# Three bias buffers, three probability buffers, and the transposes and products one unit earlier in an attention kernel

## The reference, cut to what matters

```python
# x: (16, 1024, 256), 16 heads of 16
Q, K, V = x @ Wq.T, x @ Wk.T, x @ Wv.T                 # each split into heads
rel_k, rel_v = pek[idx], pev[idx]                      # idx = clip(j - i, -256, 256) + 256
scores = (Q K^T + einsum('bhqd,qkd->bhqk', Q, rel_k)) / 4
attn = softmax(where(causal, scores, -inf))
out = attn V + einsum('bhqk,qkd->bhqd', attn, rel_v)
x = layernorm(x + out @ Wo.T)
x = layernorm(x + (silu(x @ wg.T) * (x @ wu.T)) @ wd.T)
```

## Time and profile before

| | |
|---|---|
| median of 3 runs | 5551.6 us (5548.85 to 5560.93) |
| profiled execution, its own time | 5554.04 us |
| its span | 5552.3 us |
| attention stage | about 417 to 4338 us of the span |
| TensorE, VectorE, ScalarE, GpSimd busy | 92%, 68%, 62%, 33% of the span |
| DMA | 1417.28 MB, mean 255 GB/s |

### The profile page before, as it was taken

How to read it: one execution, slowest core, us unless ns; L and a number is a source line. 1 busy time by engine, 2 the same in 40 slices (tenths; PEclk the granted TensorE clock), 3 DMA queues, 4 the chain that set the end, 5 groups by cost and what they waited for, 6 DMA issues and landing times. The chain is left out here.

```text
span 5552.3 us, 143052 instructions
## 1 busy us (share of the span) xinstructions
PE 5135.0 (92%) x49460; PEld 3335.1 (60%) x49460; DVE 3756.9 (68%) x8777; ACT 3432.3 (62%) x7512; POOL 1832.5 (33%) x2516
## 2 busy tenths in 40 slices
PE   9987999999999999999999999999999799999999
PEld 5554666666666666666666666666666465665655
DVE  4555777777777777777777777777777455555554
ACT  4446787877878778777877877787777211111111
POOL 3444333333333333333333333333333111111111
PEclk9998999999999999999999999999999899999999
DMA  7888999999999999999999999999999311111110
GB/s 225 253 254 265 318 321 320 327 320 324 326 323 322 324 325 317 326 318 317 324 324 318 324 319 318 320 324 324 320 317 312 106 61 52 54 60 60 60 54 33
DMA packets 653784, 1417.28 MB, mean 255 GB/s; under 512 B 64004, under 2 KB 362088, under 8 KB 640872
## 3 DMA queue, kind: packets, MB, share of 16 engines
q1 hardware_dynamic: 653160, 1409.10, 78.2%
HBM read 737.46 MB, written 671.35 MB: 254 GB/s over the span
## 5 line engine op out<-in xcount | busy, mean ns | idle before, releaser
L797 ACT ACTIVATE a_prob<-a_neg_s,a_neg_max 128x384 f32<-128x384 f32 (+1 forms) x1792 | 1083.3, 605 | 231.1 <-DVE a_neg_max L846 215.1
L761 PE MATMUL a_t_ps<-a_ident,a_prob 128*128 128x128 f32 x5120 | 927.8, 281 | 41.7 <-DVE a_p_t L515 28.7
L515 DVE COPY a_p_t<-a_t_ps 128x512 f32<-128x512 f32 (+3 forms) x1536 | 952.6, 620 | 6.7 <-PE a_t_ps L761 5.5
L694 PE MATMUL a_s_ps<-a_k,a_q 96*128 96x512 bf16 (+3 forms) x3072 | 853.4, 332 | 111.5 <-ACT a_far L801 106.6
L840 DVE TENSOR_REDUCE a_far_neg<-a_s_ps 128x1 f32<-128x640 f32 (+4 forms) x1280 | 707.6, 553 | 367.4 <-POOL a_bias L669 279.2
L846 DVE CUSTOM_DVE_ANT_1 a_neg_s<-a_s_ps,a_bias,a_far_neg 128x384 f32<-128x384 f32 x1280 | 791.1, 618 | 237.6 <-DVE a_far_neg L840 237.6
L804 ACT ACTIVATE a_b_out<-a_t_ps 128x512 f32<-128x512 f32 (+1 forms) x1024 | 587.6, 574 | 375.1 <-PE a_t_ps L704 363.0
L722 PE MATMUL a_o_ps<-a_p_t,a_v 128*32 128x128 f32 x18432 | 782.5, 280 | 7.1 <-ACT a_o_t L809 0.2
L801 ACT ACTIVATE a_far<-a_s_ps,a_neg_max 128x640 f32<-128x640 f32 (+4 forms) x1280 | 733.2, 573 | 0.0
L761 PE MATMUL a_t_ps<-a_ident,a_far 128*128 128x128 f32 x3840 | 668.9, 279 | 63.5 <-DVE a_p_t L515 60.9
L804 ACT ACTIVATE a_p_t<-a_t_ps 128x512 f32<-128x512 f32 (+3 forms) x1536 | 672.2, 438 | 74.6 <-PE a_t_ps L761 50.3
(11 more groups left out here) (99 smaller groups left out, 6543.4 us busy)
## 6 DMA issues: line engine op xcount, KB each, us to landing
a_bias<-bias_scr SPq DMA_DIRECT2D x448, 576.0 KB, 6.7
prob_scr<-a_prob SPq DMA_DIRECT2D x448, 576.0 KB, 6.8
bias_scr<-a_b_out SPq DMA_DIRECT2D x448, 512.0 KB, 6.9
a_band<-prob_scr SPq DMA_DIRECT2D x448, 512.0 KB, 5.7
qk_scr<-p_parts SPq DMA_DIRECT2D x256, 192.0 KB, 3.4
v_scr<-p_v_out SPq DMA_DIRECT2D x256, 128.0 KB, 2.2
a_v<-v_scr SPq DMA_DIRECT2D x64, 512.0 KB, 7.2
attn_scr<-a_o_t SPq DMA_DIRECT2D x512, 64.0 KB, 6.7
```

The lines of the kernel that those rows point to most:

```text
L515: copy(p_t[par][:, head, blocks[0] * P:(blocks[-1] + 1) * P], bank[:, 0:len(blocks) * P]) \
L694: mm = pe.matmul(s_ps[:, u % 2, c:e], q_s[0:ROWS, g, u, qb * P:(qb + 1) * P], k_s[0:ROWS, g, u, c:e], start=True, stop=True)
L761: mm = pe.transpose(bank[:, n * P:(n + 1) * P], prob_block(kk, head, b), ident[:, :])
L797: e = act.activation(near_prob(k, u, near(qb)), neg_s[:, u % 2, 0:w].rearrange("p (b c) -> p b c", c=P), ACT.Exp, bias=neg_max[:, u:u + 1] ...
```

## The change

- The bias gets a third buffer. The load of tile `k + 2` needs only the maxima of tile `k - 1`, and stands ahead of the bias saves in a step.
- The relative bias is made and saved five tiles ahead (`LEAD` 5), in eight DRAM slots. One slot of eight always belongs to the tile with `qb` 0, so its padding is laid out for short rows.
- The probabilities have three buffers instead of four; the exponentials of tile `k` wait for the save of tile `k - 3`.
- The transposes are 6 units back instead of 7: heads 2 and 3 of tile `k - 2`, then heads 0 and 1 of tile `k - 1`. The band goes to units 1 and 2, the values to units 0, 1 and 2, the relative values of tile `k - 3` to unit 3.
- The next group's q is loaded in one step, most of k in the next, the rest in a third. q and k have semaphores of their own, and the scores wait for k.

```diff
-    LEAD = 3
+    LEAD = 5
+    BIAS_SLOTS = 8
...
-        bias = sb("a_bias", [P, 2, BIAS_W])
+        bias = sb("a_bias", [P, 3, BIAS_W])
...
-        prob = sb("a_prob", [P, 4, PROB_W])
+        prob = sb("a_prob", [P, 3, PROB_W])
...
-        P_LAG = 7
-        BAND_SLOTS = ((2, 3), (3, 3))
-        VALUE_SLOTS = ((1, 3), (2, 3), (3, 3))
-        REL_SLOT = (0, 4)
-        LOADS = ((0, 0),), ((1, 0),), ((0, 1), (0, 2)), ((1, 1), (1, 2))
+        P_LAG = 6
+        BAND_SLOTS = ((1, 3), (2, 3))
+        VALUE_SLOTS = ((0, 3), (1, 3), (2, 3))
+        REL_SLOT = (3, 3)
+        LOADS = ((0, 0), (0, 1), (0, 2)), ((1, 0), (1, 1)), ((1, 2),)
...
+        def slot3(r, k):
+
+            return (TILES * r + k) % 3
...
-            for slot in range(4):
+            for slot in range(BIAS_SLOTS):
                 sp.dma_start(bias_scr[slot:slot + 1, 0:P], wide0[0:1, 0:P]).then_inc(pad_saved, 16)
-                pads = bias_scr[slot, P:P + P * WIDE].rearrange("(q c) -> q c", c=WIDE)[:, ROW:WIDE]
-                sp.dma_start(pads, wide0[:, 0:P]).then_inc(pad_saved, 16)
+                begin = 0 if q_block(slot) == 0 else ROW
+                pads = bias_scr[slot, P:P + P * WIDE].rearrange("(q c) -> q c", c=WIDE)[:, begin:WIDE]
+                sp.dma_start(pads, prob[:, 0, begin:WIDE]).then_inc(pad_saved, 16)
...
-                    if k % 2 and ok(k + LEAD):
-                        save_bias(r, k + LEAD)
                     if k + 2 >= 0 and ok(k + 2):
 
-                        par, slot = k % 2, (k + 2) % 4
-                        if ok(k):
-                            sp.wait_ge(max_ready, 4 * T + 4)
+                        par, slot = slot3(r, k + 2), (k + 2) % BIAS_SLOTS
+                        if ok(k - 1):
+                            sp.wait_ge(max_ready, 4 * T)
...
+                    if k % 2 and ok(k + LEAD):
+                        save_bias(r, k + LEAD)
...
+                if k % QB == 0 and u == 0:
+                    pe.wait_ge(k_loaded[g], 16 * 3 * (r + k // TILES + 1))
...
-                        if u == REL_SLOT[0] and ok(k - 4) and k >= 0:
-                            relative(r, k - 4)
+                        if u == REL_SLOT[0] and ok(k - 3) and k >= 0:
+                            relative(r, k - 3)
...
-                            if u == 0 and ok(k - 4):
-                                act.wait_ge(p_saved[k % 4], quad(r, k - 4))
+                            if u == 0 and ok(k - 3):
+                                act.wait_ge(p_saved[(k - 3) % 4], quad(r, k - 3))
```

More of the change, by code:

```diff
@@ L330, in attention @@
         pool_turn, dve_turn = sem("a_pool_turn"), sem("a_dve_turn")
-        qk_loaded, v_loaded = sem2("a_qk_loaded"), sem2("a_v_loaded")
+        q_loaded, k_loaded, v_loaded = sem2("a_q_loaded"), sem2("a_k_loaded"), sem2("a_v_loaded")
         b_mm, b_evac = sem("a_b_mm"), sem("a_b_evac")
-        b_saved, b_loaded = sem2("a_b_saved"), sem2("a_b_loaded")
+        b_saved, b_loaded = sem2("a_b_saved"), [sem(f"a_b_loaded{i}") for i in range(3)]
         qk_mm, far_max, max_ready, exp_ready = sem("a_qk_mm"), sem("a_far_max"), sem("a_max_ready"), sem("a_exp_ready")
@@ L368, in slots, with third, near_bias, near_prob @@
             return spread(tile[:, at:at + P], MAXD, n)
-        def near_bias(par, h, n):
+        def slot3(r, k):
+            return (TILES * r + k) % 3
+        def third(r, k):
+            return 16 * ((TILES * r + k) // 3 + 1)
+        def near_bias(r, k, h, n):
             at = B_OLD + h * MAXD + (3 - n) * B_STEP
-            return spread(bias[:, par, at:at + P], B_STEP, n)
-        def near_prob(k, h, n):
+            return spread(bias[:, slot3(r, k), at:at + P], B_STEP, n)
+        def near_prob(r, k, h, n):
             if q_block(k) == 0:
@@ L379, in near_prob, with prob_block @@
             at = X_OLD + h * MAXD + (3 - n) * X_STEP
[L380 to L382 removed]
+            return spread(prob[:, slot3(r, k), at:at + P], X_STEP, n)
+        def prob_block(r, k, h, b):
             qb = q_block(k)
@@ L389, in prob_block, with wide_prob @@
             at = X_OLD + h * MAXD + (b - qb + 2) * X_STEP
-            return prob[:, k % 4, at:at + P]
-        def wide_prob(k):
-            return prob[:, k % 4, X_RAW:X_RAW + WIDE] if q_block(k) else wide0[:, :]
+            return prob[:, slot3(r, k), at:at + P]
+        def wide_prob(r, k):
+            return prob[:, slot3(r, k), X_RAW:X_RAW + WIDE] if q_block(k) else wide0[:, :]
         def run_of(qb):
@@ L541, in load_qk @@
                     dst = (q_s, k_s)[which][first * HD:(first + count) * HD, g].rearrange("p h t -> p (h t)")
-                    sp.dma_start(dst, rows[at * HD:(at + count) * HD, :]).then_inc(qk_loaded[g], 16)
+                    sp.dma_start(dst, rows[at * HD:(at + count) * HD, :]).then_inc((q_loaded, k_loaded)[which][g], 16)
             def load_v(r, g):
@@ L562, in save_bias @@
                 n = run_of(q_block(kb))
-                rows = bias_scr[kb % 4, P:P + P * (n + P)].rearrange("(q c) -> q c", c=n + P)
+                rows = bias_scr[kb % BIAS_SLOTS, P:P + P * (n + P)].rearrange("(q c) -> q c", c=n + P)
                 sp.dma_start(rows[:, 0:n], moved_bias(kb)).then_inc(b_saved[kb % 2], 16)
@@ L584, in body @@
                         rows = prob_scr[(k - 1) % 4, 0:P * n].rearrange("(q c) -> q c", c=n)
-                        sp.dma_start(rows, wide_prob(k - 1)).then_inc(p_saved[(k - 1) % 4], 16)
-                    if k % 2 and ok(k + LEAD):
-                        save_bias(r, k + LEAD)
+                        sp.dma_start(rows, wide_prob(r, k - 1)).then_inc(p_saved[(k - 1) % 4], 16)
                     if k + 2 >= 0 and ok(k + 2):
-                        par, slot = k % 2, (k + 2) % 4
-                        if ok(k):
-                            sp.wait_ge(max_ready, 4 * T + 4)
+                        par, slot = slot3(r, k + 2), (k + 2) % BIAS_SLOTS
+                        if ok(k - 1):
+                            sp.wait_ge(max_ready, 4 * T)
                             sp.wait_ge(set_ready, SET)
-                        sp.wait_ge(b_saved[par], pair(r, k + 2))
+                        sp.wait_ge(b_saved[k % 2], pair(r, k + 2))
                         qb = q_block(k + 2)
@@ L642, in widen @@
             def widen(r, k, first, last):
-                qb, T, p = q_block(k), TILES * r + k, prob[:, k % 4]
+                qb, T, p = q_block(k), TILES * r + k, prob[:, slot3(r, k)]
                 pool.wait_ge(exp_ready, 4 * T + 4)
@@ L659, in mask @@
             def mask(r, k):
-                par, qb = k % 2, q_block(k)
-                pool.wait_ge(b_loaded[par], pair(r, k))
+                par, qb = slot3(r, k), q_block(k)
+                pool.wait_ge(b_loaded[par], third(r, k))
                 pool.sem_inc(pool_turn, 1)
@@ L761, in body @@
                                     mm = pe.transpose(bank[:, n * P:(n + 1) * P],
-                                                      prob_block(kk, head, b), ident[:, :])
+                                                      prob_block(r, kk, head, b), ident[:, :])
                                 mm.then_inc(t_mm, 1)
@@ L804, in body @@
                         read_out(act, lambda o, i: act.activation(o, i, ACT.Copy), "act", r, k, u, first, last)
[L805 to L809, removed]
+                        if u == REL_SLOT[0] and ok(k - 3) and k >= 0:
+                            act.wait_ge(o_mm, T - 2)
+                            if ok(k - 5):
+                                act.wait_ge(stored[(k - 3) % 2], pair(r, k - 5))
+                            act.activation(o_t[:, (k - 3) % 2], o_ps[:, 0:P], ACT.Copy).then_inc(o_evac, 1)
             written_out(n_iter, body)
@@ L828, in maximum @@
             def maximum(r, k, u):
-                par, qb, T = k % 2, q_block(k), TILES * r + k
+                qb, T = q_block(k), TILES * r + k
                 lo = max(0, qb - 2) * P
@@ L846, in maximum @@
                 dve.tensor_tensor_reduce(by_block(neg_s[:, u % 2, 0:w]), by_block(s_ps[:, u % 2, lo:lo + w]),
-                                         near_bias(par, u, near(qb)), -1.0, begin, ALU.add, ALU.min,
+                                         near_bias(r, k, u, near(qb)), -1.0, begin, ALU.add, ALU.min,
                                          accum_out=neg_max[:, u:u + 1]).then_inc(max_ready, 1)
```

8 lines of the change are left out of this document (4 added, 4 removed).

## The result

The changed kernel took 5633.56 us (median of 4 runs, 5630.45 to 5638.09), the kernel before 5556.05 in the same session: ratio 1.0136, 95% interval 1.0124 to 1.0148. It is 77 us slower, where 145 us less were forecast.

A forecast was written before the change was run, and what follows sets the result against it. The prediction took VectorE's wait for GpSimd's late mask to hold back the attention stage, with TensorE idle 7.1%. Terms -210 - 26 + 60 + 25 + 6 = -145 gave 5407 us, own range 5350 to 5470, over all 5300 to 5545.

The forecast's parts named there:

- the first term: Attention stage: the early bias load ends VectorE's 263.0 us of waiting for GpSimd's mask; recovered at 0.80, -210 us.
- The slope of 0.80: Pairs of heavy and light tiles: a pair gets longer by 0.80 us for 1 us more mask wait.
- upstream of both: VectorE's late start precedes TensorE's waits for transposes' copies (135.8 us) and for ScalarE's exponentials (106.6 us).
- the pair of terms for the moved units: Transposes, values, relative values one unit nearer: -26 us where VectorE bounds, +60 us for TensorE's fuller light stretch.
- The room for it: Light stretch: TensorE's waits for VectorE's copies, 0.53 us a pair, take up part of 0.9 us moved work.
- Start: Kernel start: eight more pad writes and two more bias saves, less a smaller memset; +6 us, 0 to +12.
- Bursts of q and k and the probability loop: q and k loads in two steps delay transfers up to 1.2 us; counted within the probability loop's +25 us.
- Band and three probability buffers: Band transposes a unit nearer keep 2 us of slack, three probability buffers some 6 us; both cost nothing.
- B: Rival: TensorE's 0.9 us more a pair lie bare in the light stretch; +102 us, 5650 us; chance 0.10.
- A: Rival: the DMA engines are full, so earlier loads only queue longer; 5490 us, between 5475 and 5550; chance 0.15.
- The expected mean rate of 333 GB/s: Sign of a right forecast in the profile after: the mean DMA rate rises to some 333 GB/s.

The follow-up runs named there:

- x8: x1 with the q and k loads spread over four steps instead of three (old units, bias part kept); 5514.39 us, ratio 0.9930 to the kernel before.
- x7: The kernel before with most loads of q, k and v left out from the second iteration on; 5495.13 us, ratio 0.9896.
- x2: The kernel before with only the moved units (transposes, band, values, relative values); 5657.36 us, ratio 1.0174.
- x3: The changed kernel with only the transposes back at 7 units; 5573.39 us, ratio 1.0030 to the kernel before.
- x1: The changed kernel with transposes, band, values and relative values back at old units, bias part kept; 5533.04 us, ratio 0.9954 to the kernel before.
- x5: x1 with most loads of q, k and v left out from the second iteration on; 5516.90 us, ratio 0.9933 to the kernel before.
- x6: The changed kernel with most loads of q, k and v left out from the second iteration on; 5624.08 us, ratio 1.0129 to the kernel before.
- x9: x8 with the parts of a heavy tile's values cut 3+3+2 blocks instead of 2+3+3; 5500.85 us, ratio 0.9903 to the kernel before.

## Why the prediction was wrong

**The step that failed** is the first term, "Recovered at 0.80: -210 us". The wait did go, as forecast, and it was worth some 47 us: the bias part with loads in four steps (x8) took 39 us off, 8 us of start included (45 by the stage). Other parts of the bias change are in this figure, which no run takes apart; x7, with none of them but a tenth of the bytes less, won 58 us. So 45 to 60 us came back where 210 were forecast.

The slope of 0.80 was read rightly and meant something else. Each pair was taken to end at the next heavy tile's first reduction, the very start that the mask held up, so the delay was counted in full, and what is made up in the interval behind it fell into the next pair. The kernel before shows the making up: between 1970 and 3047 us, the heavy tiles of block 6 that had waited 0.03 us on average took 2.61 us to their second reduction, those that had waited 1.25 us took 2.08. Taken from second reduction to second reduction, the same 71 pairs give 0.50 us for 1 us of wait instead of 0.80 (with a standard error of 0.06). That would still be 132 us. Why the rest didn't come either is open: most pairs had the wait (within a kind of pair the halves averaged, for one, 0.77 and 1.45 us of it), and I extended the slope down to zero, where TensorE's 2.68 us stand; but in the pairs that begin with block 7, where 8 of 17 had no wait, the slope was 0.76 as well. TensorE's stretch was within reach: the instructions of the unit are in the timeline that the earlier trace rows are from, and the change had to be costed against them. The text did know that "VectorE's late start is upstream of both" waits; it isn't what sets the time once TensorE's own unit is longer than VectorE's.

**The second** is the pair of terms for the moved units, -26 and +60, together +34; they measured +97 to +101. The work moved was rightly counted as 0.9 us a pair, and it cost 0.4. The room for it was taken to be TensorE's 0.53 us a pair of waits for copies. These did shrink, by 96 us in all, but its waits for exponentials grew by 154 us and those for the band's copies by 69. x2 shows light intervals 2.69 us longer in a group and heavy ones 1.12 shorter. The new waits were missed altogether. With transposes and values nearer, TensorE has little left in the last unit of a heavy tile and waits for the last heavy exponential. The changed kernel at that place:

```profile
2024.09 0.43 PE L746 MATMUL a_o_ps<-a_band_t,a_pv 128*32 128x128 f32 x8
2025.67 0.34 PE L706 MATMUL a_s_ps<-a_k,a_q 96*128 96x384 bf16 x1 [1.16 <-ACT a_far L813]
```

So the same move idles TensorE after the heavy maxima and fills it more in the light stretch. It takes both parts: in x3, with the values moved and the transposes not, the waits for exponentials are down to 19.5 us and those for the band's copies to 1.8, and TensorE waits 301.4 us for VectorE's copies of the transposes instead. How the 42 us of values and relative values divide between the two is not settled.

**Terms that held.** Start: forecast +6, measured +8.0 in this pair of executions; over all profiled executions the first reduction starts 6.5 us later on average with the bias part. Bursts of q and k and the probability loop: forecast +25; x1 against x8 measures the bursts at 13 us by ratios, 19 by medians. Band and three probability buffers: nothing, and no wait for the band's load (0.5 us in x2) or of ScalarE for a probability save appears. Sum of the measured terms: -47 + 8 + 13 to 19 + 101 = +75 to +81; measured +77. They must add up, as they are the differences along one chain of kernels; against the forecast, 163 us of the gap of 222 are the first term's and some 65 the second's.

**The rivals.** B, given 0.10, was the case in its sign: less than half of the wait recovered and the moved work dear, priced at 5650 against 5634. That the price is so near is in part luck. B set 0.9 us of bare work against 0.5 recovered a pair; measured are 0.4 (101/256) against 0.18 (47/256), and the start and the bursts, which B left out, add 21 to 27 us. A was wrong in its mechanism: a tenth of the bytes less won next to nothing in x5 and x6, and in x7, where it won 58 us, the mask's wait went. The expected mean rate of 333 GB/s came in no run; 326 GB/s in x8 and x9 is the highest, below the limit of some 358 GB/s that the Trainium skill's page "DMA: Bandwidth & Descriptors" gives in Specifications, so no run here tests that limit.

**What helps.** The early bias load with the old units, the loads in four steps and the values cut 3+3+2 (x9) beats both kernels: 5500.85 us, 1.0% under the kernel before.

## What to carry to other kernels

A wait on one engine is worth what it exceeds the other engines' work in the same stretch: lay the order of time of all of them side by side, and find the run of the others beside the wait before taking credit for it. A slope of time over wait must be taken between points past the one where the delay can be made up; here that brought it from 0.80 to 0.50. When stages alternate between two bounds, the same work can cost several times as much in one as in the other (64 against 16 us here), so moving work between units is a change of its own, to be timed apart; a small dose of harmless work in each place measures its price, if one looks which wait the dose itself fills.

## What was not expected of the hardware

The share of time in which DMA packets are under way hardly says how much room there is: 0.97 at 324 GB/s in x1 and 0.88 at 293 GB/s in x5 with a tenth of the bytes less came with 12 us between their times, while from 0.98 at 322 GB/s before to 0.90 at 294 GB/s in x7 there are 58 us. What counted was whether one transfer came late for the engine behind it. And latency moved from one transfer to the other and hardly changed the sum: in the changed kernel, where the bias load goes out early behind the probability save, it lands in 7.5 us instead of 6.7, and the probability save in 5.9 instead of 6.8. That the order of issue is the cause is likely, and no run changes it alone.
